# Router scores by one power on GpSimd, and opening matmuls that read a constant tile

## What is computed

```python
logits = flat @ router_w.T                      # 128 tokens x 32 experts
scores = jnp.sqrt(jax.nn.softplus(logits))
_, idx = jax.lax.top_k(scores + expert_bias, K) # K = 4
topv = jnp.take_along_axis(scores, idx, axis=1)
topv = topv / (topv.sum(axis=-1, keepdims=True) + 1e-20)
# every expert: p * (silu(clip(x @ wg.T, -7, 7)) * clip(x @ wu.T, -7, 7)) @ wd.T
```

## Time and profile before

| | |
|---|---|
| median of 3 runs | 76.15 us |
| the three runs | 74.11, 76.31, 76.15 us |
| the profiled execution | 74.17 us |
| its span, first to last instruction | 72.2 us |
| busy share of the span: PE, PEld, DVE, ACT, POOL | 93%, 68%, 62%, 57%, 59% |
| granted TensorE clock, mean | 1.00 |
| read from HBM | 15.52 MB, 217 GB/s over the span |

### The profile page before, as it was taken

How to read it: one execution, slowest core, us unless ns; L and a number is a source line. 1 busy time by engine, 2 the same in 40 slices (tenths; PEclk the granted TensorE clock), 3 DMA queues, 4 the chain that set the end, 5 groups by cost and what they waited for, 6 DMA issues and landing times.

```text
span 72.2 us, 1555 instructions
## 1 busy us (share of the span) xinstructions
PE 67.5 (93%) x552; PEld 49.4 (68%) x552; DVE 44.7 (62%) x126; ACT 40.9 (57%) x88; POOL 42.9 (59%) x50
## 2 busy tenths in 40 slices
PE   4999998999999999999999999999999999998950
PEld 1337565797864495644686888887888888897940
DVE  0058587684697627598999936634753574589520
ACT  0604556375449440459969968868960366696300
POOL 7330006150009973000799999999999999999200
PEclk9999999999999999999999999999999999999999
DMA  0899999999999499800006999999990000000002
GB/s 5 276 295 267 375 331 378 390 417 417 412 402 386 161 265 315 328 15 5 0 0 159 318 354 385 397 395 415 382 365 25 9 0 0 0 0 0 0 0 73
DMA packets 6342, 15.74 MB, mean 218 GB/s; under 512 B 704, under 2 KB 1472, under 8 KB 6336
## 3 DMA queue, kind: packets, MB, share of 16 engines
q1 hardware_dynamic: 6048, 15.39, 59.5%
q10 hardware_dynamic: 288, 0.27, 1.1%
HBM read 15.52 MB, written 0.13 MB: 217 GB/s over the span
## 4 chain that ended last, share of the span: by engine, by line
PE 68%; DVE 15%; ACT 9%; issue 4%; POOL 1%; DVEq 0%; ACTq 0%
PE bP L557 15%; PE bY L579 11%; PE bE L419 6%; PE bXT L569 5%; PE bP L356 4%; PE bY L587 4%; PE bE L557 4%; DVE gu_clip L900 3%; PE bY L408 3%; PE bXT L412 3%; PE bP L383 2%; DVE h L953 2%; DVE shifted L795 2%; ACT L727 2%; DVE row_max L793 2%
## 5 line engine op out<-in xcount | busy, mean ns | idle before, releaser
L328 POOL TENSOR_TENSOR gu_w<-gu_raw,gu_w 128x512 fp32r<-128x512 f32 x24 | 29.9, 1281 | 11.5 <-DVE gate L942 6.0
L557 PE MATMUL bP<-gu_w,xnT_parts 128*128 128x512 f32 x60 | 17.6, 428 | 0.0
L900 DVE TENSOR_SCALAR gu_clip<-bP,clip_at 128x512 f32<-128x512 f32 x13 | 10.4, 808 | 7.7 <-PE bP L557 7.7
L659 ACT ACTIVATE gu_w<-gu_raw 128x1024 fp32r<-128x1024 f32 x12 | 12.7, 1055 | 3.0 <-DMA gu_raw<-moe_w_dram 2.9
L557 PEld LDWEIGHTS bP<-gu_w,xnT_parts 128*128 128x128 f32 x60 | 11.2, 188 | 2.7 <-issue 0.5
L579 PE MATMUL bY<-dn_w,hT 128*128 128x256 f32 x40 | 10.3, 380 | 0.0
L953 DVE SCALAR_TENSOR_TENSOR h<-gu_clip,gate,bP 128x128 f32<-128x128 f32 x26 | 7.8, 340 | 0.5 <-ACT bP L734 0.4
L340 POOL TENSOR_TENSOR gu_w<-dn_w,gu_w 128x512 fp32r<-128x512 f32 x6 | 7.5, 1276 | 0.0
L579 PEld LDWEIGHTS bY<-dn_w,hT 128*128 128x128 f32 x40 | 6.8, 190 | 0.5
L740 ACT ACTIVATE hT<-bXT 128x256 f32<-128x256 f32 (+1 forms) x11 | 4.0, 366 | 4.8 <-PE bXT L569 4.8
L569 PE MATMUL bXT<-consts_sb,h 128*128 128x128 f32 x33 | 6.3, 275 | 0.3 <-DVE hT_parts L966 0.2
(11 more groups left out here) (151 smaller groups left out, 105.8 us busy)
## 6 DMA issues: line engine op xcount, KB each, us to landing
gu_raw<-moe_w_dram SPq DMA_DIRECT2D x16, 512.0 KB, 9.0
dn_w<-moe_w_dram SPq DMA_DIRECT2D x16, 256.0 KB, 8.2
aw_sb<-attn_w_dram SPq DMA_DIRECT2D x2, 512.0 KB, 7.1
shared_sb<-shared_w_dram SPq DMA_DIRECT2D x1, 384.0 KB, 12.3
small_sb<-small_dram SPq DMA_DIRECT2D x1, 370.0 KB, 7.0
xwq_sb<-x_wq_dram SPq DMA_DIRECT2D x1, 256.0 KB, 3.5
lora_sb<-lora_dram SPq DMA_DIRECT2D x1, 256.0 KB, 4.4
ctx_sb<-ctx_kv_dram ACTq DMA_DIRECT2D x1, 192.0 KB, 3.0
```

What stands on the lines that cost most here:

```text
L328: nc.gpsimd.tensor_tensor(gu_w[:, p % SLOTS, 1, cols], gu_raw[:, raw_slot(p), cols], gu_w[:, p % SLOTS, 0, cols], ALU.subtract).then_inc(g ...
L557: last = nc.tensor.matmul(bGU[n % 5][:, 0:GU], xnT_parts[:, a, k, :], gu_w[:, (n - 1) % SLOTS, w, k * GU:(k + 1) * GU], start=(k == 0 and ...
L659: nc.scalar.activation(gu_w[:, p % SLOTS, 0], gu_raw[:, raw_slot(p)], ACT.Copy).then_inc(gu_hi_ready, 1)
L900: nc.vector.tensor_scalar(gu_clip[:, n % 4, 0:width], bank[:, 0:width * 2 * I], clip_at[:, 0:1], clip_at[:, 1:2], ALU.min, ALU.max).then_i ...
```

## The change

Two things are changed.

1. The root. ACT's Ln of the softplus, DVE's `half_power`, ACT's Exp, and DVE's reciprocal, product and sum are gone. In their place POOL computes `score = softplus ^ 0.5` over 128x32 as one tensor_tensor with a tile of 0.5, between its rstd and its wait for the gate. DVE does clip 0 and clip 1 right after the softplus, then waits for the score, and `key` is score plus bias. So that the softplus is never zero, e_abs is floored at 2e-38 in the multiply that was there before. POOL's set of a 128x1 tile becomes one of 128x32.
2. The filler matmuls. They read a bf16 tile of ones that the program sets on POOL before the engines start, with a broadcast 128x512 operand. DVE's set of `warm_sb` and PE's wait for it are gone.

```diff
-            nc.gpsimd.memset(ln_floor[:], 2.0 ** -64).then_inc(powers_set, 1)
+            nc.gpsimd.memset(half[:], 0.5).then_inc(powers_set, 1)
...
                     if (p, c) == (WHOLE + 2, 0):
                         inverse_sqrt(2)
+                        pool.wait_ge(softplus_ready, 1)
+                        nc.gpsimd.tensor_tensor(score[:, 0:E], softplus[:], half[:], ALU.pow).then_inc(score_ready, 1)
                         pool.wait_ge(gate_ready, 1)
...
-                    nc.tensor.matmul(bank, warm_sb[:], warm_sb[:].unsqueeze(1).to_broadcast([128, 4, 128]),
+                    nc.tensor.matmul(bank, ones, ones_wide,
                                      start=True, stop=True, skip_group_check=True)
-            pe.wait_ge(warm_set, 1)
             keep_busy(WARM, bE[:])
...
-            act.wait_ge(softplus_ready, 1)
-            act.wait_ge(powers_set, 3)
-            nc.scalar.activation(ln_softplus[:], softplus[:], ACT.Ln, bias=ln_floor[:]
-                                 ).then_inc(ln_softplus_ready, 1)
-            act.wait_ge(half_power_ready, 1)
-            nc.scalar.activation(root[:], half_power[:], ACT.Exp, scale=0.5).then_inc(root_ready, 1)
             nc.scalar.preload_act_table(ACT.Silu)
...
-            nc.vector.memset(warm_sb[:], 1.0).then_inc(warm_set, 1)
...
-            step(nc.vector.tensor_tensor(den[:], den[:], e_abs[:], ALU.mult))
+            step(nc.vector.scalar_tensor_tensor(den[:], e_abs[:], SMALLEST, den[:], ALU.max, ALU.mult))
...
-            dve.wait_ge(ln_softplus_ready, 1)
-            nc.vector.scalar_tensor_tensor(half_power[:], logits_sb[:], -100.0, ln_softplus[:], ALU.max, ALU.min
-                                           ).then_inc(half_power_ready, 1)
             clip(1)
-            dve.wait_ge(root_ready, 1)
-            step(nc.vector.reciprocal(inv_root[:], root[:]))
-            step(nc.vector.tensor_tensor(inv_root[:], inv_root[:], softplus[:], ALU.mult))
             dve.wait_ge(zeroed, 3)
-            step(nc.vector.tensor_tensor(score2[:, 0:E], inv_root[:], root[:], ALU.add))
-            step(nc.vector.scalar_tensor_tensor(key[:, 0:E], score2[:, 0:E], 0.5, small_sb[:, EBIAS:EBIAS + E],
-                                                ALU.mult, ALU.add))
+            dve.wait_ge(score_ready, 1)
+            step(nc.vector.tensor_tensor(key[:, 0:E], score[:, 0:E], small_sb[:, EBIAS:EBIAS + E], ALU.add))
```

More of the change, by code:

```diff
@@ L43 @@
 TINY = 1e-30
+SMALLEST = 2e-38
 IDENT, HMASK = 0, 128
@@ L107, in build @@
         inv_sqrt_power = sb("inv_sqrt_power", [T, 1])
-        ln_floor = sb("ln_floor", [T, 1])
         xc = sb("xc", [T, D])
@@ L128, in build @@
         heads_outT = sb("heads_outT", [128, 2, DC, T])
-        warm_sb = sb("warm_sb", [128, 128], BF16)
+        ones = nc.const_aps.tensor(1.0, [128, 128], BF16)
+        ones_wide = nc.const_aps.tensor(1.0, [128, 512], BF16)
         logits_sb = sb("logits_sb", [T, E])
@@ L137, in build @@
         softplus = sb("softplus", [T, E])
[L138 to L142, removed]
+        half = sb("half", [T, E])
+        score = sb("score", [T, E + 1])
         key = sb("key", [T, E + K])
@@ L171, in build @@
         powers_set = sem("powers_set")
-        warm_set = sem("warm_set")
         xc_psum = sem("xc_psum")
@@ L226, in build @@
         softplus_ready = sem("softplus_ready")
-        ln_softplus_ready = sem("ln_softplus_ready")
-        half_power_ready = sem("half_power_ready")
-        root_ready = sem("root_ready")
+        score_ready = sem("score_ready")
         route_step = sem("route_step")
@@ L293, in _ @@
             nc.gpsimd.memset(inv_sqrt_power[:], -0.5).then_inc(powers_set, 1)
-            nc.gpsimd.memset(ln_floor[:], 2.0 ** -64).then_inc(powers_set, 1)
+            nc.gpsimd.memset(half[:], 0.5).then_inc(powers_set, 1)
             nc.gpsimd.memset(v_heads[:], 0.0).then_inc(zeroed, 1)
             nc.gpsimd.memset(key[:, E:E + K], SENTINEL).then_inc(zeroed, 1)
-            nc.gpsimd.memset(score2[:, E:E + 1], 2e-20).then_inc(zeroed, 1)
+            nc.gpsimd.memset(score[:, E:E + 1], 1e-20).then_inc(zeroed, 1)
             pool.wait_ge(zeroed, 3)
@@ L923, in _ @@
             clip(0)
-            dve.wait_ge(ln_softplus_ready, 1)
-            nc.vector.scalar_tensor_tensor(half_power[:], logits_sb[:], -100.0, ln_softplus[:], ALU.max, ALU.min
-                                           ).then_inc(half_power_ready, 1)
             clip(1)
-            dve.wait_ge(root_ready, 1)
-            step(nc.vector.reciprocal(inv_root[:], root[:]))
-            step(nc.vector.tensor_tensor(inv_root[:], inv_root[:], softplus[:], ALU.mult))
             dve.wait_ge(zeroed, 3)
-            step(nc.vector.tensor_tensor(score2[:, 0:E], inv_root[:], root[:], ALU.add))
-            step(nc.vector.scalar_tensor_tensor(key[:, 0:E], score2[:, 0:E], 0.5, small_sb[:, EBIAS:EBIAS + E],
-                                                ALU.mult, ALU.add))
+            dve.wait_ge(score_ready, 1)
+            step(nc.vector.tensor_tensor(key[:, 0:E], score[:, 0:E], small_sb[:, EBIAS:EBIAS + E], ALU.add))
             step(nc.vector.max(top8[:], key[:]))
             step(nc.vector.match_replace(replaced[:], top8[:], key[:], -SENTINEL))
-            step(nc.vector.scalar_tensor_tensor(weight[:], replaced[:, 0:E + 1], -SENTINEL, score2[:],
+            step(nc.vector.scalar_tensor_tensor(weight[:], replaced[:, 0:E + 1], -SENTINEL, score[:],
                                                 ALU.is_equal, ALU.mult, accum_out=weight_sum[:, 0:1]))
```

## The result

The changed kernel takes 77.65 us, the median of five runs from 76.93 to 83.08, against 74.11 for the kernel before, now also of five runs (73.7 to 76.31). The ratio is 1.044, with a 95% interval of 1.038 to 1.049: slower. Runs of either kernel fall on separate levels (74.1, 76.2 and 79.7 for the one before in later runs), and the ratio compares the lowest of each. The three runs that were known before the prediction had two on the middle level, so their median of 76.15 stood 2 us too high for the comparison.

A forecast was written before the change was run, and what follows sets the result against it. The prediction took PE to bound the kernel. From the median of 76.15 us it took off 0.25 for the opening and 0.19 for the router, together 0.44, giving 75.7 us, range 73.4 to 77.6.

The forecast's parts named there:

- D: Duration of POOL's power on 32 columns, between softplus and key: taken as some 1.3 us, bounds 0.67 and 13.6.
- The power is a loop over columns: Slower rival, at POOL's power in the router: every column pays; 2% slower from D = 3.7 us, up to 87.6; chance 0.20.
- break-even: Router: the gate is earlier than before for D under 1.94 us and later above it.
- The formula of the rival: Loop rival's time for a late gate: 76.15 - 0.25 + (D - 1.94) us, all the delay passed on; chance 0.20.
- The worth of an early gate: Router, at transpose(2): an earlier gate regains PE's whole lost 0.19 us and nothing more.
- The opening: PE's fillers, no longer waiting for DVE's set, start 0.22 to 0.32 us earlier; 0.25 taken as gain.
- goes through: Opening: the 0.25 us gain passes on to the attentions; bounds 0 to 0.32.
- 0.6 us of cover for the constants: Opening: constants land at 4.85 and the transposes of x would start at 5.44, so 0.6 us are left.
- DVE's removed set frees 0.17 us: 0: Opening, on DVE: the removed set frees 0.17 us in which DVE waits for x anyhow, worth 0.
- The middle: The forecast time for the whole kernel: 75.7 us, counted from the median of 76.15.

The follow-up runs named there:

- e8: The changed kernel run once more, unaltered, beside the kernel before on the same chip: 77.81 us median of six runs, ratio 1.051.
- e6: The changed kernel with the power on 16 columns and a multiply by 0.5 on the other 16: 74.69 us median, ratio 1.005.
- e1: The kernel before with the constant tile of ones, without DVE's set and PE's wait; router as before: 73.59 us median, ratio 0.992.
- e5: The changed kernel with nine filler matmuls in PE's idle time after gate_up(5), while the power runs: 77.24 us median, ratio to before 1.039.
- e4: The kernel before with four powers, on 2, 4, 8 and 16 columns, added in POOL's idle time after the first rstd: 74.11 us, single run.
- e10: The kernel of e1 with DVE's set of the bf16 tile put back, nobody waiting for it: 73.29 us, run once.
- e2b: The kernel of e2 measured a second time: 78.7 us median of six runs, ratio 1.057.
- e2: The changed kernel with before's set of ones and PE's wait for it put back: four runs, 80.20 to 83.04 us, ratio 1.082.

## Why the prediction was wrong, point by point

**The step that failed is the value of D.** The prediction bounded the power by 0.67 and 13.6 us, took "some 1.3 us" as "nearest to the low row", and gave the case "The power is a loop over columns" a chance of 0.20. D was 5.44. The bounds held; the choice between them had no ground, and with it fell the overlap: the power was to end about when the two clips do, and DVE waited 4.45 us for it. Plain two-input work streams at 2.15 ns a column, but that says nothing on a power, and the one row of a power showed 0.42 us over plain work for its single column. Of these 0.42, 0.16 come again with every column and 0.26 are paid once. With bounds 20 apart and a break-even at 1.94, near the low end, most of the range lay on the slower side: with equal weight for each factor of two, 65% of it is above 1.94 and 43% above 3.7.

The rule cited for that rival (the Trainium skill, GPSIMD Engine Reference, Performance pitfalls for Q7 kernels: a dependent fp32 chain pays at every step unless several are interleaved) pointed the right way, unlike the streaming row: the cost does come again with every column, 0.158 us. That such a chain inside the power is the reason is not shown, since no run here looks inside the instruction.

**The break-even of D = 1.94 was 0.4 too low.** The delay at transpose(2) is 11.58 - 8.51 = 3.07, not 5.44 - 1.94 = 3.50. Three terms make up the 0.43: the handovers to and from POOL took 0.08 more than counted (softplus to key is 5.82 in e8, D + 0.38); DVE's stall at the reciprocal was gone, -0.24, from the other edit; and from key to gate_h(2) it took 4.34 (35.96 to 40.30) in place of 4.61 (33.19 to 37.80), since both silus were long done when the gate came, -0.27. Sum: 3.07. So nothing would have been lost up to D = 2.37. This is why e6 came in under its expectation too.

**What a late gate sets off was left out.** The formula of the rival had one for one and nothing for the clock. That PE would stand idle for 1.9 us, and that the clock falls behind it in most runs, costs another 0.4 to 0.8 in these. The rows for it were at hand: the opening showed both levels.

**The worth of an early gate was right in size.** 0.19 us was read off PE's rhythm in the earlier trace rows; the multiply regained 0.23. That the other edit had regained the same 0.23 already was not foreseen. The chain of waits, which had 9 us of router in it, would have promised far more.

**The opening: the start right, the rest by luck.** Predicted 0.22 to 0.32 earlier, measured 0.28. That the gain "goes through" fits the mean (e1, 0.6 with the 0.24 of DVE's stall in it), but in the changed kernel's own profile the clock rose later against the work and the fixed point came 0.14 later than before. The "0.6 us of cover for the constants" were no cover where the clock rose during the fillers: in e5 the transposes of x stood at 5.23 and had waited for that load, which took 4.0 us. "DVE's removed set frees 0.17 us: 0" was wrong in its consequence, by the 0.24 at the reciprocal.

**The middle.** 75.7 was counted down from a median of three that lay on the middle level. From the profiled execution the same sum gives 73.7, and the rival's formula with the true D gives 74.17 - 0.25 + 3.50 = 77.4 for a result of 77.65; that it comes so near is luck, since 0.4 too much of delay stands in it for the 0.8 of the clock that it leaves out. So the start of the sum was wrong by 2 us in the direction of the result, by luck: from the right level the miss would have been 3.9 us in place of 1.9.

Of the versions that ran, the constant tile alone (e1) beats both kernels: 73.59 us, 0.992 of before.

## What to carry to other kernels

Before an operation goes to an engine on which the trace shows it at one width only, measure it at the width wanted: one added instruction in that engine's idle time, as in e4, settles in a single run what no argument from other rows could. A long step with two other steps "in its wait" is only hidden for as long as those take; here 1.35 us of clips stood against 5.44. And read from the rhythm of the bounding engine what a chain is worth before shortening it: 9 us of router were worth 0.2.

## What the runs showed of the hardware

- GpSimd's power with exponent 0.5 took 0.38 us and 0.158 us for each column of 128 partitions, from 2 to 32 columns, with a base of 0.5 throughout as with the router's values (e4, the changed kernel, e6). VectorE's wide clip beside it took 0.80 us, as without it.
- Behind an idle time of 1.67 us on PE the granted clock fell in 9 of the 11 runs of the changed kernel, and in 8 of the 10 of the root alone; the price was 0.8 us in one pair of traces and 0.4 in another. With fillers in the idle time it stayed up in 5 of 5.
- Without one DVE instruction at the head of the list, and the tile that it sets, the start of another, some 50 places on, came 0.23 us earlier (e1 against e10).
- The opening's clock rises at different moments from run to run. Read from durations, it was during the last fillers in some traces (nine fillers in 3.41 to 3.64 us), right behind them in others (4.00), near 10 us in one (e2b), which cost 2.2 us, and between 19 and 20 us in one (e2), which cost 5.4. The granted clock of the profile stands at 1.00 through all of these openings. A tenth filler did not make the late ones rarer.
